# A gated cross-attention and sparse FFN kernel: order of copies, token factors, gates and idle turns

## The chip, the cores and the metric

The kernel runs on one core of one Trainium2 chip. The metric is the device time of one execution in microseconds (us), the median of several runs.

## The reference, cut to what matters

```python
# x, ctx: (32, 128, 512) float32; mask: (32, 128) bool; w_gate, w_up: (512, 2048); w_down: (2048, 512)
def xattn(h, m, mask):
    s = einsum('bsd,bmd->bsm', h, m) / sqrt(512)
    s = where(mask[:, None, :], s, -1e30)
    out = einsum('bsm,bmd->bsd', softmax(s), m)
    return where(any(mask, -1)[:, None, None], out, 0)

def ffn(h):
    g = silu(h @ w_gate) * (h @ w_up)                  # (32, 128, 2048)
    keep, in each group of 4 neighbours, the 2 largest |g|   # 2:4 sparsity
    return g_kept @ w_down

x = x + tanh(g_xattn) * xattn(layernorm(x), ctx, mask)
x = x + tanh(g_ffn)   * ffn(layernorm(x))
```

## The kernel before, in words

Five queues run lists written out by hand, tied by semaphores: SyncE (SP, loads and stores), GpSimd (POOL), ScalarE (ACT), VectorE (DVE) and TensorE (PE). Nothing is planned by a tool; the order in the code is the order on the engine.

**Attention stage.** A loop over 39 slots n; in slot n batch n-1 is turned (four 128x128 transposes of ctx, L1340, four of the normalized x, L1345), batch n-2 gets its scores (L1353, eight passes), batch n-7 is turned for the FFN (L1361), batch n-4 is multiplied with ctx (`av`, L1367) and the probabilities of batch n-3 are turned (`pT`, L1373). ScalarE copies what was turned to SBUF, takes the exponentials and normalizes; VectorE adds the masks, takes maxima and batch statistics and makes `x1`; GpSimd makes powers and reciprocals, and with the time left converts the masks (`CONVERT`), spreads weights (`SPREAD_AT`) and takes differences (`W0_AT`, `X0_AT`). The masks are loaded by broadcast, 128 KB each; so are the two gates, 4 bytes to each of 128 partitions, and ScalarE takes their tanh in slot 3. The identity with which everything is turned is made by GpSimd (L577).

**Products.** The gate and up products are made as a two by two block scheme with seven products instead of eight (`product(u, k, e)`, k = 0 to 6, e = 0, 1), each of six matmuls in two parts: every factor is split in a high part (a rounded copy by ScalarE, `w_high`, `x_high`, `dn_high`, `h_high`) and a low part (what is left, by VectorE or GpSimd, `w_low`, `x_low`, ...). So each factor costs a copy, a subtraction and, for some, a sum (`w_sum`, `x_sum`). The order of the seven token factors is `X_TO`. There are four groups of 1024 tokens (PAIRS = 4), each with four steps s, each step with two units u = 2s and 2s+1; a unit is 14 products, 84 matmuls of about 0.227 us start to start, 19.1 us. From unit 2 on a unit is followed by half of the down product of the step before (`down`, L1399 to L1401, 48 matmuls). A few products of unit 0 stand already in slots 33 to 38 (`EARLY_AT`).

**What hangs on what in a unit.** PE's results lie in PSUM and are collected by ScalarE (`copy_a0`, `copy_a1`, `copy_d0`) and VectorE (`add_c11`, `add_c22`, `add_c12`, `gated0`, `gated1`). PE reuses the banks, so product 2 waits for `copy_a0`, product 4 for `copy_a1`, product 5 for `copy_d0`, product 6 for `add_c22`, and product 0 of the next unit for `gated0`. `x_high_at(s, point)` and `x_low_at(s, point)` put the factors of the next tokens between these. The tokens come from DRAM into `x_blk` (1 MB, L310), `dn_raw` holds raw down weights (L628, issued by GpSimd when the attention stage's stores to `xnT_scratch` have landed, because it takes their place), `w_raw` raw gate and up weights (L288).

Of the kernel before, what the change touches and what calls it, by code (L numbers as in the profile page):

```python
# [5 lines left out]
F32 = mybir.dt.float32  # L6
F32R = mybir.dt.float32r
BF16 = mybir.dt.bfloat16
U8 = mybir.dt.uint8
# [44 lines left out]
CONVERT = {1: 0, 3: 1, 4: 2, 7: 3}  # L54
# [9 lines left out]
PIECE_AT = {6: (0, 2), 7: (0, 3), 11: (1, 0), 12: (1, 1), 28: (1, 2), 29: (1, 3), 36: (2, 0), 37: (2, 1)}  # L64
SPREAD_AT = {5: ((0, 0),), 6: ((0, 1),), 10: ((0, 2),), 11: ((0, 3),), 21: ((1, 0),), 22: ((1, 1),)}
# [66 lines left out]
def flamingo_gated(nc, x, ctx, mask, g_xattn, g_ffn, w_gate, w_up, w_down, out):  # L132
# [9 lines left out]
    with whole:  # L142
# [55 lines left out]
        gates_in = sb("gates_in", [P, 2], F32, 4)  # L198
        ident = sb("ident", [P, P], F32, 4)
        x_blk1 = sb("x_blk1", [P, 4, HALF], F32, 4)  # L200
        mask_in = x1nT[:, 0, 0:2].rearrange("p c n -> p (c n)").bitcast(U8)
# [36 lines left out]
        gates_done = sem("gates_done")  # L238
# [184 lines left out]
        def _(sp):  # L423
# [52 lines left out]
            for b in range(INPUTS):  # L476
# [3 lines left out]
                if b == 4:  # L480
                    for n, g in enumerate((g_xattn, g_ffn)):
                        sp.dma_start(gates_in[:, n:n + 1], g.rearrange("(a n) -> a n", a=1)
                                     .to_broadcast([P, 1])).then_inc(gates_loaded, 16)
# [4 lines left out]
            load_mask(3)  # L488
            for n in range(SLOTS):
# [77 lines left out]
        def _(pool):  # L567
            nc.gpsimd.memset(ident[:], 0.0).then_inc(ident_set, 1)
            nc.gpsimd.memset(stats[:], 1.0).then_inc(stats_set, 1)
            nc.gpsimd.memset(least[:, 0:2], EPS)  # L570
# [88 lines left out]
        def _(act):  # L659
# [9 lines left out]

            for n in range(SLOTS):  # L670
# [21 lines left out]
                if 0 <= b < B:  # L692
# [7 lines left out]
                    else:  # L700
                        if b == 2 * TILES:
                            act.wait_ge(mask_neg_done, B // RING)
# [6 lines left out]
                if 0 <= b < B:  # L709
                    if b == 0:  # L710
                        act.wait_ge(gates_loaded, 32)
                        nc.scalar.activation(xattn_gate[:], gates_in[:, 0:1], ACT.Tanh).then_inc(gates_done, 1)
                        nc.scalar.activation(ffn_gate[:], gates_in[:, 1:2], ACT.Tanh).then_inc(gates_done, 1)
# [721 lines left out]
```

## Time and profile before

| | us |
|---|---|
| median of 3 runs | 1083.94 (1083.72 to 1084.35) |
| the profiled execution's own time | 1086.38 |
| span of its trace, first to last instruction | 1084.6 |
| PE busy | 1070.9 |
| DVE busy | 794.3 |
| ACT busy | 614.3 |
| POOL busy | 226.1 |

PE is TensorE's matmul, PEld its weight load, DVE VectorE, ACT ScalarE, POOL GpSimd, SP SyncE. A row of the timeline gives the start from the span's start, the duration, the engine, the line of the kernel, what is written and read, the count of like instructions in a row, and in brackets how long the engine had been idle and whose work ended that. A matmul's end is modelled, so the distance from one start to the next says more than its duration.

### The profile page before, as it was taken

The numbers are of one execution on the slowest core, as the hardware profiler recorded it, in microseconds if no ns is written. First come the engines' busy times: TensorE is split into PE (matmuls) and PEld (weight loads), VectorE is DVE, ScalarE is ACT, GpSimd is POOL, SyncE is SP. The second block draws the span as 40 slices with busy tenths as digits, with TensorE's granted clock in tenths as the row PEclk, the third lists the DMA queues.
The fourth block names the chain that finished last, engine by engine and source line by source line (L and its number), as shares of the span: only waits on it lengthen the run. The fifth ranks groups of instructions, "written<-read, shape, count | busy, mean of one in ns | idle before, by whom it ended". The sixth has DMA issues, their size and how long they took to land.

```text
span 1084.6 us, 15165 instructions
## 1 busy us (share of the span) xinstructions
PE 1070.9 (99%) x4972; PEld 879.4 (81%) x4972; DVE 794.3 (73%) x1389; ACT 614.3 (57%) x1126; POOL 226.1 (21%) x343
## 2 busy tenths in 40 slices
PE   7999999999999999999999999999999999999998
PEld 6888777888888888878888888878888888888887
DVE  6999879998987676676857576676856464665756
ACT  6999776777755454444544454444544444443452
POOL 7887302222111111100011111110000111111021
PEclk9999999999999999999999999999999999999999
DMA  8999985999989777787899767787798666767727
GB/s 301 323 309 323 350 355 134 329 317 289 289 268 362 174 192 189 175 271 204 241 289 285 185 177 192 180 256 203 237 306 247 153 153 155 192 151 190 199 28 144
DMA packets 89821, 252.65 MB, mean 233 GB/s; under 512 B 9104, under 2 KB 9872, under 8 KB 85648
## 3 DMA queue, kind: packets, MB, share of 16 engines
q1 hardware_dynamic: 68144, 203.45, 53.3%
q0 software_dynamic: 21600, 48.24, 26.1%
q8 instruction: 40, 0.66, 0.3%
q14 instruction: 37, 0.30, 0.1%
HBM read 153.09 MB, written 98.57 MB: 232 GB/s over the span
## 4 chain that ended last, share of the span: by engine, by line
PE 88%; DMA 4%; DVE 3%; ACT 2%; issue 1%; SPq 1%; POOL 0%; DVEq 0%; ACTq 0%; POOLq 0%
PE ps_y L1399 10%; PE ps_y L1401 10%; PE ps_y L1400 10%; PE ps_a L1326 9%; PE ps_a L1330 9%; PE ps_a L1328 9%; PE ps_d L1326 5%; PE ps_d L1330 5%; PE ps_d L1328 5%; PE ps_c L1353 3%; PE ps_y L1367 2%; PE ps_c L1330 2%; PE ps_c L1326 2%; PE ps_c L1328 2%; DMA x_blk<-xnT_scratch 2%; PE ps_a L1345 1%
## 5 line engine op out<-in xcount | busy, mean ns | idle before, releaser
L633 POOL DMA_DIRECT2D out_rows<-y_out x124 | 105.7, 856 | 707.5 <-ACT y_out L785 703.9
L1326 PE MATMUL ps_a<-xm,w_ring 128*128 128x512 f32 x512 | 200.2, 391 | 2.5 <-ACT cp L668 1.5
L1328 PE MATMUL ps_a<-xm,w_ring 128*128 128x512 f32 x512 | 199.6, 390 | 0.0
L1330 PE MATMUL ps_a<-xm,w_ring 128*128 128x512 f32 x512 | 199.5, 390 | 0.0
L785 ACT ACTIVATE y_out<-ps_y,ffn_gate 128x512 f32<-128x512 f32 x124 | 85.1, 688 | 182.7 <-PE ps_y L1401 182.7
L1399 PE MATMUL ps_y<-dn,h_hi 128*128 128x512 f32 x480 | 188.1, 392 | 0.3 <-ACT y_out L785 0.2
L1401 PE MATMUL ps_y<-dn,h_lo 128*128 128x512 f32 x480 | 187.2, 390 | 0.0
L1400 PE MATMUL ps_y<-dn,h_hi 128*128 128x512 f32 x480 | 186.7, 389 | 0.0
L762 ACT ACTIVATE h_hi<-hidden 128x512 fp32r<-128x512 f32 x128 | 73.2, 625 | 82.7 <-DVE hidden L1095 82.6
L1069 DVE TENSOR_TENSOR beats<-h_abs 128x512 bf16<-128x512 f32 x186 | 117.7, 684 | 1.3 <-ACT h_abs L755 1.3
L1326 PEld LDWEIGHTS ps_a<-xm,w_ring 128*128 128x128 f32 x512 | 96.1, 188 | 24.8 <-issue 3.0
L1330 PEld LDWEIGHTS ps_a<-xm,w_ring 128*128 128x128 f32 x512 | 96.1, 188 | 20.3
L1328 PEld LDWEIGHTS ps_a<-xm,w_ring 128*128 128x128 f32 x512 | 96.1, 188 | 20.0
L1037 DVE TENSOR_TENSOR cp<-ps_c,cp 128x512 f32<-128x512 f32 x64 | 43.7, 690 | 90.6 <-PE ps_c L1330 90.6
L1399 PEld LDWEIGHTS ps_y<-dn,h_hi 128*128 128x128 f32 x480 | 90.1, 188 | 21.3 <-ACT y_out L785 2.8
L1401 PEld LDWEIGHTS ps_y<-dn,h_lo 128*128 128x128 f32 x480 | 90.1, 188 | 19.3
L1400 PEld LDWEIGHTS ps_y<-dn,h_hi 128*128 128x128 f32 x480 | 90.1, 188 | 18.9
L1326 PE MATMUL ps_d<-xm,w_ring 128*128 128x512 f32 x256 | 100.0, 391 | 1.6 <-ACT hidden L738 1.5
L1330 PE MATMUL ps_d<-xm,w_ring 128*128 128x512 f32 x256 | 99.7, 389 | 0.0
L1328 PE MATMUL ps_d<-xm,w_ring 128*128 128x512 f32 x256 | 99.6, 389 | 0.0
L755 ACT ACTIVATE h_abs<-hidden 128x512 f32<-128x512 f32 x124 | 74.1, 625 | 28.2 <-DVE hidden L1061 28.2
L1043 DVE TENSOR_TENSOR hidden<-ps_a,hidden 128x512 f32<-128x512 f32 x64 | 43.6, 689 | 57.3 <-PE ps_a L1330 56.8
(122 smaller groups left out, 1872.4 us busy)
## 6 DMA issues: line engine op xcount, KB each, us to landing
w_ring<-w_scratch SPq DMA_DIRECT2D x147, 512.0 KB, 4.3
out_rows<-y_out POOLq DMA_DIRECT2D x124, 256.0 KB, 4.2
w_scratch<-w_ring SPq DMA_DIRECT2D x56, 512.0 KB, 5.9
xm_scratch<-x_out SPq DMA_DIRECT2D x40, 512.0 KB, 5.5
xm<-xm_scratch SPq DMA_DIRECT2D x19, 1024.0 KB, 7.4
w_raw<-in_L_ffn_w_down SPq DMA_DIRECT2D x9, 1024.0 KB, 7.8
x_in<-in_x SPq DMA_DIRECT2D x32, 256.0 KB, 5.2
ctx_in<-in_ctx SPq DMA_DIRECT2D x32, 256.0 KB, 5.4
```

What stands on the lines that cost most here:

```text
L633: nc.gpsimd.dma_start(out[RING * (n // (2 * TILES * QS)) + TILES * ORDER[order] + n % TILES], y_out[:, n % 4], accum_op=ALU.add).then_inc( ...
L755: nc.scalar.activation(abs_of(s, order)[:, j], hidden[:, h, j], ACT.Abs).then_inc(abs_done, 1)
L762: nc.scalar.activation(h_hi[:, h, j], hidden[:, h, j], ACT.Copy).then_inc(h_hi_done, 1)
L785: nc.scalar.activation(y_out[:, n % 4], ps_y[n % 2][:], ACT.Identity, scale=ffn_gate[:]).then_inc(y_copied, 1)
L1037: nc.vector.tensor_tensor(cp[:, e, 0], ps_c[e][:], cp[:, e, 0], ALU.add).then_inc(c11_done[e], 1)
L1069: nc.vector.tensor_tensor(beats[:, PAIR[i, j]], abs_of(s, order)[:, i], abs_of(s, order)[:, j], ALU.is_ge).then_inc(beats_done, 1)
L1326: nc.tensor.matmul(to, w_ring[:, k, e, 0, c], xm[:, k, 0, c], start=begins and c == 0, stop=False, skip_group_check=not begins)
L1328: nc.tensor.matmul(to, w_ring[:, k, e, 0, c], xm[:, k, 1, c], start=False, stop=False, skip_group_check=not begins)
L1330: last = nc.tensor.matmul(to, w_ring[:, k, e, 1, c], xm[:, k, 0, c], start=False, stop=c == 1, skip_group_check=not begins)
L1399: nc.tensor.matmul(to, h_hi[:, h, j, at], right[:, 0, j, columns], start=at_j == 0, stop=False)
L1400: nc.tensor.matmul(to, h_hi[:, h, j, at], right[:, 1, j, columns], start=False, stop=False)
L1401: last = nc.tensor.matmul(to, h_lo[:, h, j, at], right[:, 0, j, columns], start=False, stop=at_j == GROUP - 1)
```

## The change

Seven edits: (1) PE's first three slots are written out in another order, with 12, 10 and 6 transposes of the identity between them, whose result nobody reads; (2) the gates are loaded to one partition by ScalarE's queue and spread by a product with a row of ones; (3) the last eight token factors of the first group are made in slots 30 to 37 instead of 29 to 36, the low halves of the last two on VectorE in unit 0; (4) the four masks lie in the place of `xm`'s last product instead of `x1nT`'s, and the fourth is loaded in slot 14 and converted in slot 21, with spreads and weight pieces moved to make room; (5) the last weight piece and `x_blk` are loaded behind the last `xnT_scratch` store; (6) `copy_a1` and `copy_d0` stand ahead of `dn_high`, spreads and `x_high_at`, and VectorE's `x_low_at(s, 0)` behind `add_c22` in all steps; (7) in unit 0 `gated0` comes ahead of the second `add_c12`.

```diff
-CONVERT = {1: 0, 3: 1, 4: 2, 7: 3}
+CONVERT = {1: 0, 3: 1, 4: 2, 21: 3}
-PIECE_AT = {6: (0, 2), 7: (0, 3), 11: (1, 0), 12: (1, 1), 28: (1, 2), 29: (1, 3), 36: (2, 0), 37: (2, 1)}
-SPREAD_AT = {5: ((0, 0),), 6: ((0, 1),), 10: ((0, 2),), 11: ((0, 3),), 21: ((1, 0),), 22: ((1, 1),)}
+PIECE_AT = {6: (0, 2), 8: (0, 3), 12: (1, 0), 13: (1, 1), 28: (1, 2), 30: (1, 3), 36: (2, 0)}
+SPREAD_AT = {5: ((0, 0),), 7: ((0, 1),), 10: ((0, 2),), 11: ((0, 3),), 22: ((1, 0),), 29: ((1, 1),)}
-         | {29 + 2 * (i - 3) + k: (k, i) for i in range(3, 7) for k in range(2)})
+         | {30 + 2 * (i - 3) + k: (k, i) for i in range(3, 7) for k in range(2)})
+IDLE_TURNS = (12, 10, 6)
...
@@ SP
-                if b == 4:
-                    for n, g in enumerate((g_xattn, g_ffn)):
-                        sp.dma_start(gates_in[:, n:n + 1], g...to_broadcast([P, 1])).then_inc(gates_loaded, 16)
-            load_mask(3)
+                if n == 14:
+                    load_mask(3)
-                if n == SLOTS - 3:
-                    load_x_blk(sp, 1, 0)
+            load_w_piece(sp, nc.sync, 2, 1)
+            load_x_blk(sp, 1, 0)
@@ ACT
+            for n, g in enumerate((g_xattn, g_ffn)):
+                nc.scalar.dma_start(gates_in[:, n:n + 1], g.rearrange("(a n) -> a n", a=1)).then_inc(gates_loaded, 16)
-                        act.wait_ge(gates_loaded, 32)
+                        act.wait_ge(gates_spread, 1)
@@ ACT, step s > 1, first unit
-                        x_high_at(s, 0)
                         copy_d0(u, 0)
                         copy_d0(u, 1)
+                        x_high_at(s, 0)
@@ ACT, unit 1
-                    dn_high(0, 0)
-                    dn_high(0, 1)
                     copy_a1(1, 0)
                     copy_a1(1, 1)
-                    dn_high(0, 2)
-                    dn_high(0, 3)
-                    x_high_at(0, 1)
-                    spread(act, 2, 3)
+                    for j in range(GROUP):
+                        dn_high(0, j)
                     copy_d0(1, 0)
                     copy_d0(1, 1)
+                    spread(act, 2, 3)
+                    x_high_at(0, 1)
@@ ACT, unit 3
+                if s == 1:
+                    copy_d0(u, 0)
+                    copy_d0(u, 1)
                 if building:
                     spread(act, u + 1, 1)
                 x_high_at(s, 2)
-                copy_d0(u, 0)
-                copy_d0(u, 1)
+                if s > 1:
+                    copy_d0(u, 0)
+                    copy_d0(u, 1)
@@ DVE
-                if n == SLOTS - 2:
-                    dve.wait_ge(x_lo_done, 13)
-                    x_low(dve, nc.vector, 0, *X0_AT[n - 1])
-                    if s > QS:
-                        x_low_at(s, 0)
                     add_c22(u, 0)
                     add_c22(u, 1)
                     if s <= QS:
                         dn_low(dve, nc.vector, s - 1)
-                        x_low_at(s, 0)
+                    x_low_at(s, 0)
@@ DVE, unit 0
                     add_c11(0, 1)
+                    dve.wait_ge(x_lo_done, 12)
+                    x_low(dve, nc.vector, 0, 0, 6)
+                    x_low(dve, nc.vector, 0, 1, 6)
                     add_c12(0, 0)
+                    gated0(0, 0)
                     add_c12(0, 1)
+                    gated0(0, 1)
                     w_low(dve, nc.vector, 1, 5)
-                    gated0(0, 0)
-                    gated0(0, 1)
@@ PE (turn_ctx, turn_x and score are the loop's old parts)
+            def idle_turns(count):
+                for i in range(count):
+                    nc.tensor.transpose(ps_av[0][:, 0:P], ident[:], ident[:])
+            idle_turns(IDLE_TURNS[0])
+            turn_ctx(0)
+            idle_turns(IDLE_TURNS[1])
+            turn_x(0)
+            turn_ctx(1)
+            score(0)
+            idle_turns(IDLE_TURNS[2])
+            turn_x(1)
+            turn_ctx(2)
+            score(1)
+            turn_x(2)
+            pe.wait_ge(ones_set, 1)
+            pe.wait_ge(gates_loaded, 32)
+            nc.tensor.matmul(ps_av[1][:, 0:2], ones[:], gates_in[:], start=True, stop=True).then_inc(gates_spread, 1)
+            for n in range(3, SLOTS):
```

## Rows read from the trace of the kernel before

**Rows 1.** The page, busy us (share of the span) and instructions.

```profile
PE 1070.9 (99%) x4972; PEld 879.4 (81%) x4972; DVE 794.3 (73%) x1389; ACT 614.3 (57%) x1126; POOL 226.1 (21%) x343
```

**Rows 2.** Chain of waits at the start: start us, us, what.

```profile
10.61 1.71 PE ps_c L1353 x8
...
16.45 0.89 PE ps_c L1353 x8
```

**Rows 3.** Timeline of the start: start, us, engine, line, operation, count, idle before.

```profile
1.25 0.28 POOL L577 TENSOR_SCALAR_AFFINE_SELECT ident<-ident 128x128 f32<-128x128 f32 x1
...
4.22 1.08 PE L1340 MATMUL ps_a<-ident,ctx_in 128*128 128x128 f32 x4 [4.22 <-DMA ctx_in<-in_ctx]
...
6.81 1.11 PE L1345 MATMUL ps_a<-ident,xn 128*128 128x128 f32 x4 [1.51 <-ACT xn L688]
...
12.75 0.29 DVE L1011 TENSOR_REDUCE neg_max<-neg_scores 128x1 f32<-128x129 f32 x1
...
15.09 0.33 PE L1373 MATMUL ps_d<-ident,probs 128*128 128x128 f32 x1
```

**Rows 4.** Busy us of PE, PEld, DVE, ACT, POOL in a stretch; clock, DMA, GB/s.

```profile
40.00:60.00 20.00, 20.00 (x149) 16.83 (x148) 19.55 (x51) 19.46 (x50) 18.02 (x33) 1.00 0.88 308
```

**Rows 5.** Timeline behind the attention stage, and one stretch as in rows 4.

```profile
117.24 1.30 POOL L390 TENSOR_TENSOR xm<-x_blk,xm 128x512 fp32r<-128x512 f32 x1
...
117.62 0.48 PE L1326 MATMUL ps_a<-xm,w_ring 128*128 128x512 f32 x1
...
122.60 0.53 SPq L499 DMA_DIRECT2D xnT_scratch<-x1nT  x1
...
127.23 0.69 DVE L347 TENSOR_TENSOR w_ring<-w_blk,w_ring 128x512 fp32r<-128x512 f32 x1 [1.45 <-ACT w_ring L343]
...
128.00:136.00 8.00, 7.50 (x34) 5.92 (x33) 7.15 (x12) 5.88 (x9) 1.76 (x3) 1.00 1.04 407
```

**Rows 6.** Timeline of PE, unit 1: the matmuls after waits.

```profile
132.93 0.47 PE L1326 MATMUL ps_a<-xm,w_ring 128*128 128x512 f32 x1 [0.49 <-DVE hidden L1055]
...
145.55 0.47 PE L1326 MATMUL ps_a<-xm,w_ring 128*128 128x512 f32 x1 [1.47 <-ACT cp L668]
...
155.08 0.47 PE L1326 MATMUL ps_a<-xm,w_ring 128*128 128x512 f32 x1 [0.25 <-DVE hidden L1055]
```

**Rows 7.** Timeline of ACT, unit 1, and one issue of POOL.

```profile
134.77 0.63 ACT L385 ACTIVATE x_out<-x_blk 128x512 fp32r<-128x512 f32 x1 [1.37 <-DMA xnT_scratch<-x1nT]
...
135.21 0.59 POOL L628 DMA_DIRECT2D dn_raw<-in_L_ffn_w_down  x1 [4.78 <-DMA xnT_scratch<-x1nT]
...
137.50 1.12 ACT L333 ACTIVATE w_blk<-w_raw 128x512 f32<-128x512 f32 x1 [0.60 <-DMA w_raw<-in_L_ffn_w_up]
...
141.14 0.62 ACT L343 ACTIVATE w_ring<-w_blk 128x512 fp32r<-128x512 f32 x1
...
143.77 1.15 ACT L775 ACTIVATE dn<-dn_raw 128x512 fp32r<-128x512 f32 x2 [2.02 <-DMA dn_raw<-in_L_ffn_w_down]
...
146.82 0.63 ACT L385 ACTIVATE x_out<-x_blk 128x512 fp32r<-128x512 f32 x1
```

**Rows 8.** Timeline of DVE, unit 1.

```profile
148.52 0.69 DVE L353 TENSOR_TENSOR w_blk<-w_blk 128x512 f32<-128x512 f32 x1 [0.18 <-ACT w_blk L333]
...
154.25 0.68 DVE L1055 TENSOR_TENSOR hidden<-ps_a,cp 128x512 f32<-128x512 f32 x1
```

**Rows 9.** Timeline of PE and ACT, units 3 and 12.

```profile
200.06 0.47 PE L1326 MATMUL ps_d<-xm,w_ring 128*128 128x512 f32 x1 [0.30 <-ACT hidden L738]
...
469.57 0.64 ACT L385 ACTIVATE x_out<-x_blk 128x512 fp32r<-128x512 f32 x1 [4.14 <-DMA x_blk<-xnT_scratch]
...
470.83 0.47 PE L1326 MATMUL ps_d<-xm,w_ring 128*128 128x512 f32 x1 [0.59 <-ACT hidden L738]
...
482.16 0.50 PE L1399 MATMUL ps_y<-dn,h_hi 128*128 128x512 f32 x1 [0.17 <-ACT y_out L785]
```

**Rows 10.** The tile x_blk, all six loads.

```profile
DMA to landing us min/median/max: 9.0/9.9/10.5
```

More of the change, by code:

```diff
@@ L722, in _ @@
                 if n in X0_AT:
+                    if X0_AT[n] == (0, 6):
+                        act.wait_ge(mask_neg_done, B // RING)
                     x_high(act, 0, *X0_AT[n])
@@ L1332, in product @@
                 last.then_inc(made[k], 1)
-            for n in range(SLOTS):
-                b = n - 1
-                if 0 <= b < B:
-                    pe.wait_ge(ctx_in_loaded[b % INPUTS], 16 * (b // INPUTS + 1))
-                    wait(pe, cT_copied, b)
-                    for c in range(KC):
-                        last = nc.tensor.transpose(ps_cT[:, c], ctx_in[:, b % INPUTS, c * P:(c + 1) * P], ident[:])
-                    last.then_inc(cT_done, 1)
-                    pe.wait_ge(xn_done, b + 1)
-                    wait(pe, xT_copied, b)
-                    for c in range(KC):
-                        last = nc.tensor.transpose(ps_xT[:, c], xn[:, b % 2, c * P:(c + 1) * P], ident[:])
-                    last.then_inc(xT_done, 1)
-                b = n - 2
-                if 0 <= b < B:
-                    pe.wait_ge(xT_copied, b + 1)
-                    pe.wait_ge(cT_copied, b + 1)
-                    wait(pe, neg_scores_done, b - 1)
-                    for c in range(KC):
-                        last = nc.tensor.matmul(ps_sc[b % 2][:, 0:M], xnT[:, b % 2, c], ctxT[:, b % 2, c],
-                                                start=(c == 0), stop=(c == KC - 1))
-                    last.then_inc(scores_done, 1)
@@ new lines, in turn_ctx, with turn_x @@
+            def turn_ctx(b):
+                pe.wait_ge(ctx_in_loaded[b % INPUTS], 16 * (b // INPUTS + 1))
+                wait(pe, cT_copied, b)
+                for c in range(KC):
+                    last = nc.tensor.transpose(ps_cT[:, c], ctx_in[:, b % INPUTS, c * P:(c + 1) * P], ident[:])
+                last.then_inc(cT_done, 1)
+            def turn_x(b):
+                pe.wait_ge(xn_done, b + 1)
+                wait(pe, xT_copied, b)
+                for c in range(KC):
+                    last = nc.tensor.transpose(ps_xT[:, c], xn[:, b % 2, c * P:(c + 1) * P], ident[:])
+                last.then_inc(xT_done, 1)
@@ new lines, in score @@
+            def score(b):
+                pe.wait_ge(xT_copied, b + 1)
+                pe.wait_ge(cT_copied, b + 1)
+                wait(pe, neg_scores_done, b - 1)
+                for c in range(KC):
+                    last = nc.tensor.matmul(ps_sc[b % 2][:, 0:M], xnT[:, b % 2, c], ctxT[:, b % 2, c],
+                                            start=(c == 0), stop=(c == KC - 1))
+                last.then_inc(scores_done, 1)
+            def idle_turns(count):
+                for i in range(count):
+                    nc.tensor.transpose(ps_av[0][:, 0:P], ident[:], ident[:])
@@ L1356, in _ @@
+            for n in range(3, SLOTS):
+                if 3 < n <= B:
+                    turn_ctx(n - 1)
+                    turn_x(n - 1)
+                if 3 < n < B + 2:
+                    score(n - 2)
                 b = n - 7
@@ L1366, in _ @@
                     wait(pe, x1_done, b - 1)
+                    if b == 1:
+                        pe.wait_ge(gates_done, 2)
                     nc.tensor.matmul(ps_av[b % 2][:], probsT[:, b % 2], ctx_in[:, b % INPUTS], start=True,
```

16 lines of the change are left out of this document (7 added, 9 removed).

## The prediction

> **What bounds the kernel now.** I read the page's busy shares first: PE is busy 1070.9 us of a span of 1084.6 [rows 1]. So no edit that shortens work beside TensorE is worth anything by itself, and at most the 13.7 us in which PE stands can be won. The chain of waits and the timeline of the start show where much of it lies: PE does nothing until 4.22, stands again before 6.81, and reaches its first transposed probabilities only at 15.09 [rows 3]. After that it is full: every 20 us stretch of the attention stage has PE busy 20.00, with ScalarE and VectorE near 19.5 [rows 4]. For the rest I looked along PE's timeline for places where two neighbouring matmuls start further apart than the usual 0.23 us. There are nine such waits of 0.3 us or more that the change can touch: four in unit 1 of the gate and up products (three of them in [rows 6], the fourth at 149.11), one at 200.06, and two pairs of the kind of 470.83 and 482.16 [rows 9], the second pair at 711.89 and 723.22. Below, a wait is counted from start to start less 0.23, and 0.08 is added, because the matmul after a restart is that much slower to follow.
>
> **Part 1, the start: idle turns, another order, gates by TensorE.** Before, PE's clock is at its low level here. The granted clock reads 1.00 in the windows view here too, as in [rows 4], but eight matmuls of the scores take 1.71 us at 10.61 and 0.89 us at 16.45 [rows 2]: 1.2 GHz first, 2.4 GHz later, and what preceded the rise was PE's first stretch without a pause. A turn of 128x128 is thus 0.213 us low and 0.11 us high. The identity is ready at 1.53 (1.25 + 0.28) [rows 3]. Twelve idle turns take 2.56 us from some 1.75 on, so they end at 4.3, when the first context's turns were to begin at 4.22: hidden. Ten more follow at 5.15 and end at 7.3 if the clock is still low; x's turns started at 6.81, so they are up to 0.48 late. I take the clock to be up by about 8, since PE then has worked without a pause since 1.75. Then the scores of batch 0 end at 9.45, six idle turns (0.66) at 10.1, x's second turns run 10.1 to 10.55, x's copy and the next xn follow on ScalarE, the scores of batch 1 end at 12.2, and x's third turns at 12.65, about 1.3 earlier than before. Next in line is probs of batch 0: it needs the maximum, which VectorE ends at 13.04 whatever PE does [rows 3], because its own input is held by the loads. So pT starts at about 13.85 instead of 15.09: 1.24 at best. With a rise at 8.6 I get 0.85, with one after 10.6 nothing, and with the rise where it is now a loss of 1.2 (every added turn stands at 0.213 and x's second turns wait for them). Value: 1.1, ends 1.25 and -1.2. The gates' two broadcast loads leave SP's queue and are issued by ScalarE before its first work, in the time in which it waits for the statistics; the tanh reads the same two columns from PSUM. One small matmul for them stands after x's third turns. Cover for both is that wait; without it they would cost under 1 us once, and I take nothing. The fourth mask load goes from the full first queue to slot 14, its conversion (GpSimd, slot 7 to 21) and the spreads that make room keep one such job a slot; PE is full there, so nothing.
>
> The Trainium skill, "TensorE: Matmul & The Clock Gate", section "Part 1: The HAM clock gate", says the moment of the rise is not tied to the kernel's start and differs from run to run. This trace has one execution and cannot show that; by the rule the term of the start would be between -1.2 and 1.25 from run to run, and the median of runs would hide a part of it. It is the first rival below.
>
> **Part 2, the token factors' sums a slot later.** The eight last token factors move from slots 29 to 36 to slots 30 to 37. The early products on PE keep their slots. The product that needs factor 5 (place 2) starts at 117.62 [rows 5]. That factor's low half is now the one that GpSimd makes at 117.24 for 1.30 us, so it is ready at 118.54 where PE would begin at 117.7: PE stands 0.9. Against it, VectorE has one sum of 128x512 fewer (0.6 to 0.7, as in [rows 8]) before slot 32, and it is full there, so GpSimd's job comes up to 0.6 earlier. Ends -0.9 and -0.3 (not below nothing: PE takes products in order, and the factor cannot be earlier than its copy). Value: -0.4. The two last low halves move behind c11 on VectorE, 1.2 us there; VectorE waits 1.45 for ScalarE behind them before 127.23 [rows 5], which hides them.
>
> **Part 3, unit 1.** The four waits are 0.73, 1.71, 0.83 and 0.49 us (the matmuls before them start at 132.05, 143.69, 148.13 and 154.44) [rows 6]. The first is behind gated0, which now comes one addition earlier: gone. The second and third are copies of ScalarE behind dn's high parts, which wait for dn_raw until 143.77 [rows 7], and behind a spread: both gone as such. But what comes late next? VectorE has a fixed list before gated0 of unit 1, on which PE's next unit waits. It is busy without a pause from 148.52 to 154.25 [rows 8], and its list starts when ScalarE is through with dn's parts, a spread and x_high. ScalarE has no pause from 137.50, where a weight load lands, to its last w_high at 141.14, behind which it is free at 141.66 [rows 7]. From there the new order is two copies (0.95), four dn parts (0.53 each, 2.1), two copies (0.95), the spread (1.04): x_high at 146.70 instead of 146.82 [rows 7], but with all else done. VectorE then has its x_low at 147.37 and its list at 147.97 instead of 148.52. So PE's four waits of 3.76 become one of about 3.2 before unit 2, and the gain is only 0.55. This needs dn_raw by 142.6. It lands at 143.77 now, 8.5 after 135.21, because GpSimd issues it when the last xnT store, issued at 122.60, has landed [rows 5, 7]; that store will have 1.5 MB (x_blk and a weight piece) behind it instead of in front, 3.9 us at 407 GB/s [rows 5], so dn_raw comes by about 140. If it does not, the term is -0.5; if the 0.60 wait at 137.50 [rows 7] goes too, 1.15.
>
> What is moved back pays. x_blk was issued at about 120.5 and is now behind the store, and behind the low half of factor 6, at about 124.6. The loads of x_blk land 9.0 to 10.5 us after issue [rows 10], so at 134.1 to 135.6. ScalarE's x_high waits for it; it ran at 134.77 [rows 7], and 0.60 of slack follows, so up to 135.4 costs nothing. I take nothing; the end is -0.2.
>
> **Part 4, the later units.** At 200.06 copy_d0 now precedes a spread and x_high: the wait of 0.54 goes, but VectorE's x_low, which stands before its c22, comes 0.95 later and c22 is just in time. Value 0.4, ends 0.1 and 0.54. At 470.83 copy_d0 stood behind an x_high that waited 4.14 us for x_blk [rows 9]; now only x_high waits. VectorE's x_low moves behind c22 for the same reason. The wait of 0.83 goes. The one at 482.16 (0.44) comes from the same delay: ScalarE is about 1 us earlier at dn's parts and VectorE 0.5, so it goes too. The pair at 711.89 and 723.22 is 0.38 and 0.40. Sum 1.27 + 0.78 = 2.05, ends 0.8 (only the direct waits go, partly) and 2.05. In the other steps copy_d0 can wait up to 0.8 for PE before x_high; ScalarE is about half idle there, so nothing.
>
> **Sum.** 1.1 - 0.4 + 0.55 + 0.4 + 2.05 = 3.7 us. The profiled execution took 1086.38 (span 1084.6) and would take 1082.7; the three runs have the median 1083.94, so 1080.2.
>
> **Rivals.** (a) The clock rises as late as now. For it: the rise is an observation of one execution; against it: PE is without a pause much earlier. Term 1 is then -1.2: 1082.5. (b) The waits of ScalarE and VectorE only change place: units 1 and later give nothing, because each engine's list stays as long. For it: exactly this happens to most of part 3; against: at 470 ScalarE stood 4.14 us for a load, with nothing else late [rows 9]. Gain 0.7: 1083.2. (c) Unit 1's waits all go, if VectorE's list starts earlier than ScalarE's order allows by my count: 3.2 more, 1077.0. (d) The slower one: x_blk. Both engines' lists in unit 1 hang on ScalarE's x_high at about 134.8. Each us of its landing past 135.4 moves PE by one; from 139.1 the whole gain of 3.7 is lost. A landing at 141.6, 17 us after issue, gives 1086.4. For it: the xnT store before it needed 12 us in this queue (122.60 to about 134.7) [rows 5, 7]; against: all six x_blk loads needed 10.5 or less [rows 10].
>
> **Numbers.** Forecast 0.60, (a) 0.15, (b) 0.12, (c) 0.07, (d) 0.06. The range 1078.9 to 1083.0 holds the forecast with its bounds, (a), and leaves out (b)'s half, (c) and (d). A difference under 0.2% (2.2 us) can't be told from none here. Faster by more needs a time under 1081.8: most of the forecast, (c), a little of (a): 0.66. Within: 0.27. Slower: 0.07.
>
> **What would show it.** Part 1: the first pT before 14.3, scores of batch 0 in 0.9 us. Part 2: PE standing 0.3 to 0.9 before its place 2 product. Part 3: no wait inside unit 1 and one of about 3 us before unit 2. Part 4: no wait at the five later places. Wrong would be: unit 2 starting as late as now after the shift of the start, x_high of ScalarE waiting past 135.4 for x_blk, or new waits above 0.3 us after unit 3.

## The result, and the profile after

The changed kernel takes 1088.48 us (median of 6 runs, 1087.27 to 1089.47) against 1084.58 for the kernel before in the same session: ratio 1.0035, 95% interval 1.0023 to 1.0046. It is slower by 3.9 us; the forecast was 1080.2, faster by 3.7, and the time lies outside its range.

The profiled execution of the changed kernel took 1087.74 (span 1085.9), that of before 1086.38 (span 1084.6). So the two traces differ by 1.3 us where the medians differ by 3.9. A comparison of these two traces alone would mislead; the second profile of before, below, is needed.

**The start.** PE's timeline, columns as in [rows 3]:

```profile
6.86 0.65 PE L1348 MATMUL ps_a<-ident,xn 128*128 128x128 f32 x4
...
8.20 1.16 PE L1356 MATMUL ps_c<-ctxT,xnT 128*128 128x128 f32 x8
9.20 0.82 PE L1363 MATMUL ps_y<-ident 128*128 128x128 f32 x6
...
14.26 0.33 PE L1405 MATMUL ps_d<-ident,probs 128*128 128x128 f32 x1 [1.22 <-ACT probs L685]
```

Scores run at the high level from the first batch on: its eight passes take 1.0 us, from 8.20 to 9.20, where they took 1.71 before [rows 2]. The first pT comes at 14.26 instead of 15.09, and PE stands 1.22 before it. The forecast had 13.85, because it took VectorE's maximum to end at 13.04 as before [rows 3]. It ended at 13.68, behind a load of x that VectorE had at 10.83 (at 10.13 in the trace of before):

```profile
10.83 0.69 DVE L1034 BATCH_NORM_STATS2 bn<-x_in 128x6 f32<-128x512 f32 x1 [2.35 <-DMA x_in<-in_x]
...
13.39 0.29 DVE L1013 TENSOR_REDUCE neg_max<-neg_scores 128x1 f32<-128x129 f32 x1
```

**Place 2 and unit 1.** GpSimd's low half of factor 5, then PE's timeline; these rows answer to [rows 5] and [rows 6]:

```profile
116.41 1.27 POOL L393 TENSOR_TENSOR xm<-x_blk,xm 128x512 fp32r<-128x512 f32 x1
...
117.78 0.47 PE L1329 MATMUL ps_a<-xm,w_ring 128*128 128x512 f32 x1 [0.75 <-issue]
...
150.27 0.47 PE L1329 MATMUL ps_a<-xm,w_ring 128*128 128x512 f32 x1 [1.39 <-DVE hidden L1045]
...
154.67 0.47 PE L1329 MATMUL ps_a<-xm,w_ring 128*128 128x512 f32 x1 [1.42 <-DVE hidden L1057]
```

ScalarE and VectorE in the same stretch; they answer to [rows 7] and [rows 8]:

```profile
142.80 2.19 ACT L778 ACTIVATE dn<-dn_raw 128x512 fp32r<-128x512 f32 x4
144.88 1.07 ACT L741 ACTIVATE hidden<-ps_d 128x512 f32<-128x512 f32 x2
145.84 1.11 ACT L336 ACTIVATE w_blk<-w_raw 128x512 f32<-128x512 f32 x1
146.84 0.64 ACT L388 ACTIVATE x_out<-x_blk 128x512 fp32r<-128x512 f32 x1
```

```profile
147.50 0.69 DVE L393 TENSOR_TENSOR x_out<-x_blk,x_out 128x512 fp32r<-128x512 f32 x1 [1.55 <-ACT x_out L388]
148.11 0.69 DVE L356 TENSOR_TENSOR w_blk<-w_blk 128x512 f32<-128x512 f32 x1
...
149.44 1.28 DVE L1045 TENSOR_TENSOR hidden<-ps_a,hidden 128x512 f32<-128x512 f32 x2
```

The low half is done at 117.68 and PE starts place 2 at 117.78; the row of PE names no releaser for its 0.75. The four waits of unit 1 are gone and two new ones of about 1.6 each (start to start) have come, both for VectorE: one inside the unit, at 150.27, and one before unit 2. ScalarE has dn's parts, copy_d0 and the spread ahead of x_high, which so comes as late as before, at 146.84 (146.82 before). The low half of that factor stands first in VectorE's list, so VectorE waits 1.55 for x_high, and only then does its list go on.

**Step 7.** First VectorE of before, then of after, in the stretch before the second half of down:

```profile
528.82 0.68 DVE L390 TENSOR_TENSOR x_out<-x_blk,x_out 128x512 fp32r<-128x512 f32 x1
529.42 0.69 DVE L403 TENSOR_TENSOR x_blk<-x_blk 128x512 f32<-128x512 f32 x1
530.20 0.69 DVE L1043 TENSOR_TENSOR hidden<-ps_a,hidden 128x512 f32<-128x512 f32 x1
...
539.71 1.28 DVE L1048 TENSOR_TENSOR cp<-ps_d,cp 128x512 f32<-128x512 f32 x2
```

```profile
529.11 0.69 DVE L1045 TENSOR_TENSOR hidden<-ps_a,hidden 128x512 f32<-128x512 f32 x1 [1.30 <-PE ps_a L1333]
...
531.08 0.68 DVE L393 TENSOR_TENSOR x_out<-x_blk,x_out 128x512 fp32r<-128x512 f32 x1
531.68 0.68 DVE L406 TENSOR_TENSOR x_blk<-x_blk 128x512 f32<-128x512 f32 x1
...
539.82 1.28 DVE L1050 TENSOR_TENSOR cp<-ps_d,cp 128x512 f32<-128x512 f32 x2
```

Before, x_low and x_sum (1.2 us together) stood where VectorE waits for PE's product anyway. After, VectorE idles 1.30 there and does them behind c22, in a list without a gap: dn's low parts, the counts, keep, c12. So c12 ends where it did, although PE arrives 1.1 us earlier. PE pays:

```profile
536.03 0.50 PE L1431 MATMUL ps_y<-dn,h_hi 128*128 128x512 f32 x1 [0.15 <-DVE dn L321]
...
542.39 0.50 PE L1431 MATMUL ps_y<-dn,h_hi 128*128 128x512 f32 x1 [0.63 <-ACT y_out L788]
```

The same pair stands at 778.23 and 784.59 (step 11). In steps 6 and 10 the waits ahead of the down product, at 481.04 and 723.24, are 0.60 each. At 470.83, 711.89 and 200.06 PE no longer waits, as forecast for [rows 9].

**The kernel before, profiled again.** A second profile of it has PE at the start, and ScalarE in unit 12, as follows:

```profile
13.84 1.55 PE L1353 MATMUL ps_c<-ctxT,xnT 128*128 128x128 f32 x8
15.22 0.27 PE L1373 MATMUL ps_d<-ident,probs 128*128 128x128 f32 x1
```

```profile
469.00 0.63 ACT L385 ACTIVATE x_out<-x_blk 128x512 fp32r<-128x512 f32 x1 [3.59 <-DMA x_blk<-xnT_scratch]
```

x_blk landed half a microsecond earlier than in [rows 9], and PE's wait at 470 was 0.21 instead of 0.75; the pair at 711.89 and 723.22 was not there. This execution took 1085.18. The waits that part 4 was to remove are thus partly an accident of the first profile: of the experiments below with ScalarE's order of before, e3, e10 and e11 have 0.53 to 0.57 at 470, e12 has 0.35, and e2, e5, e8, e9 and e13 have under 0.2.

Where PE starts some units, in each trace (us):

| kernel | unit 3 | unit 4 | unit 13 | unit 15 | unit 23 | end |
|---|---|---|---|---|---|---|
| before | 185.87 | 216.55 | 487.75 | 547.88 | 788.92 | 1084.56 |
| before, again | 185.79 | 216.50 | 487.21 | 547.34 | 787.70 | 1083.38 |
| after | 185.41 | 215.98 | 486.66 | 548.02 | 790.22 | 1085.87 |
| e1 | 185.32 | 215.88 | 486.62 | 546.97 | 787.92 | 1083.55 |
| e2 | 185.26 | 215.96 | 486.64 | 547.97 | 791.04 | 1086.71 |
| e3 | 186.37 | 217.39 | 488.36 | 548.49 | 789.40 | 1085.06 |
| e6 | 183.72 | 215.86 | 485.94 | 546.29 | 787.06 | 1082.72 |
| e7 | 184.29 | 216.44 | 486.71 | 547.08 | 788.65 | 1084.28 |
| e8 | 183.99 | 214.66 | 484.75 | 544.87 | 785.51 | 1081.18 |
| e10 | 183.54 | 214.22 | 485.25 | 545.38 | 785.97 | 1081.65 |

After and e2 lose 1.2 us between units 13 and 15 against all others, and again before unit 23.

### The profile page after: what moved, and what is told of

Same layout as the page of the kernel before. It is cut to its first block, busy times and chain, and to the rows that moved or that the text cites. A ratio compares the mean times of both kernels' runs of the same rounds, so it can differ in the third digit from the quotient of the medians.

```text
span 1085.9 us, 15227 instructions
## 1 busy us (share of the span) xinstructions
PE 1073.4 (99%) x5002; PEld 881.6 (81%) x5002; DVE 794.7 (73%) x1390; ACT 614.3 (57%) x1126; POOL 225.6 (21%) x343
## 4 chain that ended last, share of the span: by engine, by line
PE 90%; DVE 4%; issue 2%; ACT 2%; DMA 1%; SPq 0%; POOL 0%; DVEq 0%; ACTq 0%; POOLq 0%
PE ps_y L1431 10%; PE ps_a L1329 10%; PE ps_y L1433 10%; PE ps_y L1432 10%; PE ps_a L1331 10%; PE ps_a L1333 10%; PE ps_d L1329 5%; PE ps_d L1331 5%; PE ps_d L1333 5%; PE ps_c L1329 3%; PE ps_c L1333 3%; PE ps_c L1331 3%; PE ps_y L1399 3%; PE ps_c L1356 2%; PE ps_a L1348 1%
```

## The experiments

The ratio is to the kernel before, from runs on the same chip, with its 95% interval. Medians of different sessions differ by some tenths for the same kernel, so I compare ratios; 0.001 is 1.1 us.

| kernel | median | ratio, interval |
|---|---|---|
| after | 1088.48 | 1.0035, 1.0023 to 1.0046 |
| e1 after, x_low back | 1086.81 | 1.0018, 1.0010 to 1.0027 |
| e2 before, x_low behind c22 | 1088.53 | 1.0032, 1.0020 to 1.0044 |
| e3 before, the start alone | 1086.56 | 1.0007, 0.9999 to 1.0016 |
| e4 after, no idle turns | 1089.40 | 1.0043, 1.0027 to 1.0058 |
| e5 e1, part 4 back | 1084.88 | 1.0006, 0.9997 to 1.0015 |
| e6 e1, ScalarE's unit 1 back | 1084.86 | 1.0000, 0.9992 to 1.0009 |
| e7 e1, slots back | 1085.40 | 1.0002, 0.9993 to 1.0010 |
| e8 e1, all three back | 1083.03 | 0.9982, 0.9973 to 0.9991 |
| e9 e8, y first | 1082.58 | 0.9981, 0.9971 to 0.9991 |
| e10 before, loads alone | 1083.28 | 0.9987, 0.9978 to 0.9996 |
| e11 e10, copy_d0 first in step 1 | 1083.34 | 0.9985, 0.9976 to 0.9995 |
| e12 e9, new order in unit 1 | 1083.02 | 0.9978, 0.9969 to 0.9987 |
| e13 e10, with the start | 1083.19 | 0.9984, 0.9975 to 0.9992 |

**e1 and e2: VectorE's x_low.** e1 undoes the edit in the changed kernel, e2 makes it alone in the kernel before:

```diff
-                    if s > QS:
-                        x_low_at(s, 0)
                     add_c22(u, 0)
                     add_c22(u, 1)
                     if s <= QS:
                         dn_low(dve, nc.vector, s - 1)
-                        x_low_at(s, 0)
+                    x_low_at(s, 0)
```

> The changed kernel, with VectorE's x_low and x_sum of the steps after the fourth put back ahead of its two c22 additions. Theory L (the loss is VectorE's: its x_low and x_sum, 1.2 us together, now stand behind c22 and delay keep, silu1 and the copies of y): the waits near 536 and 542 and near 778 and 785 go (2 x 1.1 to 1.3 us), of those at 470 and 711 up to 1.0 comes back, so 1088.5 - 1.5 = 1087.0 (1086.0 to 1087.5), and PE has no wait over 0.3 us near 536 and 542. Rival A (ScalarE's order, copy_d0 ahead of x_high, makes them): both pairs of waits stay and the time stays within 0.5 of 1088.5. Rival S (the loss is at the start, which the traces hide because the profiled execution of before was one of its slow ones): the waits may go, but the time stays over 1087.5.

> The kernel before, with this one part of the change: VectorE's x_low and x_sum behind c22 in the steps after the fourth. Theory L: the waits near 536, 542, 778 and 785 appear and the time is 1084.6 + 2.5 = 1087.1 (1086.0 to 1087.5). Rival A: no such waits, 1084.6 within 0.5. Rival S: 1084.6 within 0.5.

Alone, the edit makes the kernel before slower: ratio 1.0032 (1.0020 to 1.0044), 3.5 us, where theory L had 2.5 and at most 1087.5. Its trace has the waits of the changed kernel at the same places, those ahead of the down product in steps 6 and 10 too (0.60 and 0.76):

```profile
542.37 0.50 PE L1397 MATMUL ps_y<-dn,h_hi 128*128 128x512 f32 x1 [0.63 <-ACT y_out L785]
```

Undone in the changed kernel, the ratio goes from 1.0035 to 1.0018. What PE waits for from 125 to 1050, us in total, times, longest, first after, then e1:

```profile
PE ps_y L1431 <- ACT y_out L788: 2.2, 4, 0.6
PE ps_a L1329 <- DVE hidden L1057: 1.4, 1, 1.4
PE ps_a L1329 <- DVE hidden L1045: 1.4, 1, 1.4
PE ps_y L1431 <- DVE dn L321: 0.3, 2, 0.2
```

```profile
PE ps_a L1331 <- DVE hidden L1045: 1.4, 1, 1.4
PE ps_a L1331 <- DVE hidden L1057: 1.4, 1, 1.4
PE ps_y L1433 <- ACT y_out L788: 0.5, 2, 0.2
```

So theory L holds, rival A (ScalarE's order makes these waits) falls: e1 keeps that order. The cost is 1.8 to 3.5 us by the ratios and 2.3 by the traces of after and e1, of which 0.6 arises in steps 6 and 10 (0.18 and 0.38 in e1 instead of 0.60 each). The profiled execution of e1, 1085.41, is its fastest. Rival S is not excluded for the rest: e1 is still slower than before.

**e3 and e4: the start.** e3 is the kernel before with the idle turns, the order of the first turns and the gates by TensorE; e4 is the changed kernel without the turns.

```diff
# e3, onto the kernel before
-                                     .to_broadcast([P, 1])).then_inc(gates_loaded, 16)
+                nc.scalar.dma_start(gates_in[:, n:n + 1], g.rearrange("(a n) -> a n", a=1)).then_inc(gates_loaded, 16)
+            idle_turns(IDLE_TURNS[0])
...
# e4, onto the changed kernel
-IDLE_TURNS = (12, 10, 6)
+IDLE_TURNS = (0, 0, 0)
```

> The kernel before, with the start of the changed one alone: idle turns, the order of the first turns and scores, and the gates by ScalarE's two loads and a matmul. The mask loads stay where they were. Theory L with the start as the two traces show it: pT of batch 0 comes 0.8 us earlier, 1084.6 - 0.8 = 1083.8. Rival S (the clock of the kernel before rises early in most of its executions, so that the idle turns only stand in the way): 1085.6 to 1087, slower than before.

> The changed kernel with no idle turns, all else as it is. If the turns bring what the two traces show, this is 0.8 us slower than the changed kernel, 1089.3. Rival S: 1.0 to 2.5 us faster than it, 1086.0 to 1087.5, with the first pT earlier than 14.26.

e3 brings its first pT to 13.85, 1.2 earlier than before, and is not faster: 1.0007; its median lies where rival S had it, its pT does not. Its trace shows the loss in unit 1: the wait for dn_raw is longer and TensorE's clock falls behind it. PE's timeline, and then PE's granted clock (the figure 0.75) in a stretch, columns as in [rows 4]:

```profile
145.88 0.67 PE L1327 MATMUL ps_a<-xm,w_ring 128*128 128x512 f32 x1 [2.62 <-ACT cp L667]
146.34 0.63 PE L1329 MATMUL ps_a<-xm,w_ring 128*128 128x512 f32 x1
146.77 0.63 PE L1331 MATMUL ps_a<-xm,w_ring 128*128 128x512 f32 x1
```

```profile
140.00:144.00 4.00, 3.26 (x15) 2.37 (x13) 1.28 (x2) 0.83 (x2) 0.00 (x0) 1.00 1.01 410
144.00:148.00 4.00, 2.12 (x5) 1.72 (x6) 2.52 (x5) 3.90 (x8) 0.00 (x0) 0.75 1.03 417
148.00:152.00 4.00, 4.00 (x16) 3.20 (x15) 3.76 (x7) 1.82 (x3) 0.72 (x1) 0.83 0.94 351
```

After a wait of 2.62 us eight matmuls follow each other at 0.43 us, the low level, instead of 0.23: 1.6 us on top of the wait. Not all of it is lost, since the two waits of before that follow, 0.75 and 0.41, are gone: 0.4 to 0.5 is left. The mean granted clock of a run shows such an execution as 0.998 or 0.997: 7 of the 11 runs of e3, and 9 of the 104 runs of before that stand beside the experiments; those nine took 1085.4 to 1088.2. The four runs of e3 without it took 1085.6 to 1086.7 and are not faster than before either. The wait itself takes most of the gain: dn_raw is issued at 134.30, 0.9 earlier than before, but lands at 144.08, 0.3 later. So an earlier start made a wait for an unmoved load longer, and in most runs the clock added to it. e4 says little about the idle turns: its two slowest runs (1092.7) have the low clock too, and its interval overlaps that of after. In its trace the clock rises at 10.6 without them and pT comes at 14.53 (after: 14.26); it loses 2.0 at a wait near 212, on which more below. Its expectation (1089.3) was met in the number, for other reasons.

**e5, e6, e7: one part undone each, from e1.** e5 puts ScalarE's x_high ahead of copy_d0 again in all later steps; e6 undoes ScalarE's order of unit 1,

```diff
-                    copy_a1(1, 0)
-                    copy_a1(1, 1)
-                    for j in range(GROUP):
-                        dn_high(0, j)
-                    copy_d0(1, 0)
-                    copy_d0(1, 1)
-                    spread(act, 2, 3)
-                    x_high_at(0, 1)
+                    dn_high(0, 0)
+                    dn_high(0, 1)
+                    copy_a1(1, 0)
+                    copy_a1(1, 1)
+                    dn_high(0, 2)
+                    dn_high(0, 3)
+                    x_high_at(0, 1)
+                    spread(act, 2, 3)
+                    copy_d0(1, 0)
+                    copy_d0(1, 1)
```

and e7 puts the token factors in slots 29 to 36 again, with VectorE's last low half where it was. The diffs of e5 and e7:

```diff
                         copy_a1(u, 1)
+                        x_high_at(s, 0)
                         copy_d0(u, 0)
                         copy_d0(u, 1)
-                        x_high_at(s, 0)
...
                 x_high_at(s, 2)
-                if s > 1:
-                    copy_d0(u, 0)
-                    copy_d0(u, 1)
+                copy_d0(u, 0)
+                copy_d0(u, 1)
```

```diff
-         | {30 + 2 * (i - 3) + k: (k, i) for i in range(3, 7) for k in range(2)})
+         | {29 + 2 * (i - 3) + k: (k, i) for i in range(3, 7) for k in range(2)})
```

Beside them stands b_again, the kernel before, unchanged: the second profile shown above.

> The first experiment's kernel (VectorE's x_low back in front of c22), and ScalarE's x_high again ahead of copy_d0 in all later steps, as before the change. Theory P (part 4 of the forecast holds for ScalarE's order): the waits near 199.5, 470 and 711 come back, 1.0 to 1.4 us in all, 1086.8 + 1.2 = 1088.0. Rival Q (with VectorE's x_low ahead of c22 the order of ScalarE decides nothing, since c22 waits for x_low and that for x_high): 1086.8 within 0.4.

> The first experiment's kernel with ScalarE's order in unit 1 as before the change (dn's parts ahead of and between the copies, x_high ahead of the last spread); VectorE's order and the loads stay. By the traces unit 1 stood 3.4 us before and 3.1 after. Theory V (unit 1 hangs on VectorE's list, which starts at ScalarE's last spread and x_high whatever stands before them): 1086.8 within 0.5, waits of 3.1 to 3.6 in unit 1. Rival W (the order itself was the gain): waits of 4 or more, 1087.8 or more.

> The first experiment's kernel with the token factors again in slots 29 to 36, and VectorE's last low half where it was. The wait of 0.9 at the product of place 2 goes. Theory G (what is won ahead of unit 1 is given back there, since ScalarE's and VectorE's lists of unit 1 start from a weight load that lands at 137.5): the waits of unit 1 grow by what place 2 gained, unit 3 starts where it did (185.3), 1086.8 within 0.4. Rival H (it counts): 1085.9, unit 3 at 184.4.

> The kernel before, unchanged, for a second profile of it. The one at hand was of an execution of 1086.4, the median is 1085.1. Theory N (dn_raw lands earlier in other executions): the first pT again at 15.1, and the wait at 145.5 of 1.6 shorter, 0.3 to 1.0, unit 3 at 184.6 to 185.3. Rival S (TensorE's clock rises earlier in other executions): scores of batch 0 in 0.9 us, first pT before 14.3.

All three came out faster than e1, e6 clear of its interval, where theory P had e5 slower, Q, V and G had e5, e6 and e7 the same within 0.4 or 0.5, and W had e6 slower. Only rival H, for e7, came near (1085.9, unit 3 at 184.4). e5: its trace has the wait at 199.69 back (0.49), as P says, but none at 470 and 711. e6: unit 3 starts at 183.72 instead of 185.32, and unit 1 has waits of 0.35, 0.71 and 0.40 instead of 1.61 and 1.56. With the loads moved, the old order of ScalarE is the better one by 1.6 us: its x_high comes at 144.71 instead of 146.72, because copy_d0 and the spread no longer stand ahead of it. e7: the wait of 0.91 at place 2 is gone and unit 3 starts 1.03 earlier; nothing was given back in unit 1. Both traces lose it again later, at one wait (unit 4 starts at 215.86 in e6 and 216.44 in e7, at 215.88 in e1):

```profile
210.24 0.50 PE L1435 MATMUL ps_y<-dn,h_hi 128*128 128x512 f32 x1 [1.45 <-ACT y_out L788]
```

ScalarE and GpSimd of e6 show why:

```profile
207.46 1.11 ACT L336 ACTIVATE w_blk<-w_raw 128x512 f32<-128x512 f32 x1 [3.27 <-DMA w_raw<-in_L_ffn_w_up]
208.47 1.13 ACT L758 ACTIVATE h_abs<-hidden 128x512 f32<-128x512 f32 x2
209.51 1.25 ACT L788 ACTIVATE y_out<-ps_y,ffn_gate 128x512 f32<-128x512 f32 x2
```

```profile
198.03 0.76 POOL L291 DMA_DIRECT2D w_raw<-in_L_ffn_w_up  x1 [4.28 <-ACT w_blk L336]
```

The copies of y stand behind a spread whose weights land 9.4 us after their issue at 198.03, and this issue waits for an earlier spread. Of b_again, theory N was right on the first pT alone: dn_raw landed at 143.70, the wait at 145.5 was 1.56, not shorter, and unit 3 started at 185.79. What was smaller were the waits at 470 and 711, of which N said nothing. Rival S finds nothing in this profile.

**e8, e9, e10.** e8 undoes all three parts together from e1. e9 adds ScalarE's first copy of y ahead of the two absolute values:

```diff
                     spread(act, u + 1, 3)
+                    copy_y(s - 1, 1, 0)
                 for j in second:
                     absolute(s, 0, j)
```

e10 is the kernel before with three lines of part 3:

```diff
-... 36: (2, 0), 37: (2, 1)}
+... 36: (2, 0)}
-                if n == SLOTS - 3:
-                    load_x_blk(sp, 1, 0)
+            load_w_piece(sp, nc.sync, 2, 1)
+            load_x_blk(sp, 1, 0)
...
                     add_c12(0, 0)
+                    gated0(0, 0)
                     add_c12(0, 1)
+                    gated0(0, 1)
                     w_low(dve, nc.vector, 1, 5)
-                    gated0(0, 0)
-                    gated0(0, 1)
```

> All of ScalarE's orders in units 1 and later and the token factors' slots as before the change, with VectorE's x_low back too; what stays of the change are the start, the places of the weight pieces, masks and x_blk, and gated0 one addition earlier. If each undone part counts by itself: unit 3 starts at 182.8, the time is 0.9990 of before, 1083.9. Theory G2 (a gain ahead of unit 3 is given back near 210, where the copies of y stand behind a spread of ScalarE whose weights land at 207 to 208 whatever came before): a wait of 1.5 to 2.4 near 210, 1084.6, as in the kernel with unit 1 alone undone.

> The kernel with three parts undone, and ScalarE's first copy of y ahead of the two absolute values (1.04 us) in the second halves of the first steps. Theory G2: the wait near 210 is 1.0 shorter than in the kernel with three parts undone and the time 1.0 less, 1083.6 or less. Rival (PE waits there for VectorE or for the weights themselves): the wait and the time are the same within 0.3.

> The kernel before, with three lines of part 3 alone: x_blk and the weight piece behind the last xnT store, and gated0 one addition earlier. Theory D (unit 1 of before waits for dn_raw, whose issue waits for that store): dn_raw is issued at 131 instead of 135, the waits of unit 1 are 1.5 instead of 3.4, unit 3 starts at 184.0. The time is then 1.6 less than before, 1083.4, or, by theory G2, 0.3 to 0.6 less with a wait near 211. Rival: dn_raw lands as late as before (the engines that move data are full) and nothing changes.

All three beat the kernel before. e10, by 1.4 us (0.9987, 0.9978 to 0.9996), bears theory D out. It moves two loads and also `gated0`, so the 1.4 is for the three together: the wait of 0.65 at 132.93, which hung on `gated0`, is gone too. Its issue of dn_raw:

```profile
130.13 0.59 POOL L628 DMA_DIRECT2D dn_raw<-in_L_ffn_w_down  x1
```

against 135.21 before [rows 7], and PE's waits from 125 on, which are no longer for dn_raw's chain (`cp L668`, 1.5 before, 0.2 now):

```profile
PE ps_d L1326 <- ACT hidden L738: 1.3, 3, 0.6
PE ps_a L1326 <- DVE hidden L1055: 0.3, 1, 0.3
PE ps_a L1326 <- DVE w_ring L347: 0.2, 1, 0.2
PE ps_a L1326 <- ACT cp L668: 0.2, 1, 0.2
```

dn_raw was issued 5.1 earlier and landed 2.8 earlier, at 140.99. e8 is faster than its expectation by the ratio, though its unit 3 starts at 183.99 and not 182.8: there dn_raw landed 12.4 us after its issue, and PE waited 1.44 for a copy behind it at 143.68. It had no wait near 210, so theory G2 falls as I put it: the landing is not at a fixed time. With the spread ahead of copy_d0 the piece is issued at 197.36, 13.37 behind the start of unit 3 (e6: 14.31), and ScalarE has it at 205.33. e9 could not show a gain where the wait was already gone; its ratio is that of e8.

**e11, e12, e13.** e11 is e10 with copy_d0 ahead of the spread and x_high in step 1; e12 is e9 with spread, copy_d0, x_high in unit 1 in this order and VectorE's x_low behind c22 there; e13 is e10 with the start of e3.

```diff
# e11
+                if s == 1:
+                    copy_d0(u, 0)
+                    copy_d0(u, 1)
                 if building:
                     spread(act, u + 1, 1)
...
# e12, ScalarE
-                    x_high_at(0, 1)
                     spread(act, 2, 3)
                     copy_d0(1, 0)
                     copy_d0(1, 1)
+                    x_high_at(0, 1)
# e12, VectorE
-                    x_low_at(0, 1)
                     w_sum(dve, 2, 0)
                     w_sum(dve, 2, 1)
                     add_c22(1, 0)
                     add_c22(1, 1)
+                    x_low_at(0, 1)
```

> The kernel with the loads of part 3 alone, and one more edit: in the second half of step 1 ScalarE's copy_d0 ahead of the spread and x_high, as the change has it. Theory R (that order takes the wait of 0.5 at 197.8 and gives more back: the spread, and with it the issue of the weight piece that ScalarE needs before the copies of y, comes 0.95 later): the issue is 14.3 behind the start of unit 3 instead of 13.4, PE waits 0.2 to 1.6 near 210, the time is 0 to 1.2 above the kernel with the loads alone, 1084.0. Rival (part 4 as forecast): the wait at 197.8 goes and nothing comes, 1082.9.

> The kernel with three parts undone and the copy of y first, with one new order in unit 1: ScalarE's last spread and copy_d0 ahead of its x_high, VectorE's x_low behind c22. The wait of 0.7 before the product of place 5 (copy_d0 behind x_high and the spread) should shrink to 0.2 and unit 3 start 0.4 to 0.6 earlier, at 182.8: 1082.1. Rival V (unit 1 hangs on the length of VectorE's list only): the waits change place, unit 3 at 183.3, 1082.6.

> The kernel with the loads of part 3 alone, and the start of the change: idle turns, order, gates by TensorE. On its own the start brought nothing (ratio 1.0007). Theory D2 (its gain was lost in unit 1, which waited for dn_raw; with dn_raw issued early it counts): 0.5 to 1.0 less than the kernel with the loads alone, 1082.5. Rival S (the clock of the kernel with the old start rises by itself at 10 in many executions, pT at 14.0, so that the turns bring nothing): 1083.3 within 0.4.

e11: the issue came 14.3 behind unit 3 as theory R says, the wait at 197.8 was gone, and none came near 210, since the piece was there at 204.60. The time is that of e10 (0.9985 and 0.9987). So the order costs only in executions in which that load is slow. All sixteen traces fit this. With copy_d0 first, the issue is 14.3 behind unit 3: where the piece landed 7.8 to 7.9 after its issue (after, e1, e11) PE did not wait near 210, and where it landed 9.4 to 9.8 after (e4, e6, e7) PE waited 1.6 to 2.0. With the spread first, the issue is 13.4 behind, and no wait there was over 0.22, though the landing took up to 9.3 (e3, and e9 and e12, which also have the copy of y first). That the load was slow in most runs of e1 is argued, not shown. e12: the wait before place 5 fell from 0.72 in e9 to 0.20, and that before unit 2 grew from 0.41 to 1.01. The waits changed place, as rival V says, though unit 3 started later than either text had it, at 184.08; the ratio, 0.9978, is not told apart from 0.9981. Its x_high comes at 146.95, as late as in the changed kernel, yet VectorE's list goes on at 146.13, because x_low stands behind c22 there. e13: the start on top of the loads is worth 0 to 0.3 us (0.9984 against 0.9987), so theory D2 (0.5 to 1.0) falls and rival S holds, and the traces say why. The first pT comes at 13.72 in e13; with the old start it comes at 15.09, 15.22 and 15.19 (before, its repetition, e2), but at 14.01 in e10 and 13.71 in e11. PE's timeline of e10:

```profile
10.03 1.11 PE L1353 MATMUL ps_c<-ctxT,xnT 128*128 128x128 f32 x8
...
14.01 0.33 PE L1373 MATMUL ps_d<-ident,probs 128*128 128x128 f32 x1 [0.83 <-ACT probs L682]
```

The eight scores start 0.94 before the next turns, nearly all at the high level: the clock rose at 10.1, with code that is the same up to here as that of before, where it rose at 14.0. In e10 PE had paused until 9.12, 1.0 before the rise; in before it had worked without a pause for 4.6, which is what the prediction saw ahead of the rise. Hence rival S, which b_again seemed to refute, is true in part. By the rule of the Trainium skill that the prediction weighed ("TensorE: Matmul & The Clock Gate", section "Part 1: The HAM clock gate": the moment of the rise differs from run to run) this is expected, and these traces agree: five profiles of one start gave rises from 10.1 to 14.9. The half microsecond to either side that the page gives for it is too little here.

## Why the prediction was wrong, step by step

- **The step that failed** is in part 4: "VectorE's x_low moves behind c22 for the same reason" and "In the other steps ... nothing". I looked at step 6 alone, where x_high waited 4.14 us for x_blk [rows 9], and costed steps 7 and 11 at nothing from ScalarE's idle share. But the list that moved is VectorE's. In steps 7 and 11 it carries an x_sum besides, and the low parts of dn for the same half, so behind c22 there is no gap, while ahead of c22 there is one of 1.3 us. In steps 6 and 10, where the move was taken for a gain, it costs 0.6. Cost in all: 1.8 us by e1, 3.5 by e2, 2.3 by the traces.
- **A second step failed with it**: ScalarE's new orders and the slots stand in parts 2 to 4, which were put at a gain of 2.6 in all. Undoing the orders and slots gains 3.9 by the ratios (e1 to e8), twice what undoing x_low does from after to e1.
- **Part 4, the gain of 0.4 + 2.05.** Three of the five waits went, at 200.06, 470.83 and 711.89, but of the two profiles of before only the one that I read had 0.5 of the 0.75 at 470.83 and the pair at 711.89. The two ahead of the down product grew, at 481.04 and 723.24 (0.60 each, 0.33 and 0.29 before); by e1 and e2 that is x_low's doing. And e5 puts ScalarE's order at a cost of 1.3 instead: behind copy_d0 the spread, and with it the issue of the next weight piece, comes 0.9 later.
- **Part 3, 0.55.** My count of ScalarE's list was right (x_high at 146.70 forecast, 146.84 measured), and the waits of unit 1 went from 3.44 to 3.13, 0.3 instead of 0.55. One of the two left is inside the unit, where I had none. dn_raw landed at 141.57, 10.9 after its issue, where I had taken 8.5 and "about 140"; it was in time all the same. What I missed is what the same loads give with the old order: 1.6 us more (e6). I compared the new order only with the old order and the late dn_raw. Once dn_raw is there in time, copy_d0 and the spread ahead of x_high hold it back by 2.0, and that costs VectorE 1.55 of idle time.
- **Part 2, -0.4.** The wait was 0.91, the end of my range that I had not taken; e7 puts its price at 1.0 in the trace and 1.7 by the ratio.
- **Part 1, 1.1.** 0.83 in this trace. Over all traces the first pT comes at 13.71 to 15.22 with the old start and at 13.72 to 14.44 with the new one, so the term is -0.7 to 1.5 from one execution to the next. Rival (a) did not happen: the clock rose at 5.8 here, and by 7.8 in every trace with the idle turns. What varies is the start of the kernel before, which I had at a fixed time. Where the start does come earlier and the loads stay, as in e3, the wait for dn_raw takes it.
- **Rivals.** (d) did not happen: x_blk landed 9.3 us after its issue and ScalarE took it without a wait. (b), that the waits of ScalarE and VectorE change place, is what happened to unit 1, but it was put at a gain, where a list that is moved out of a gap is a loss. None of my rivals had the place that decided. The range was narrower than its own terms, too: their worst ends (-1.2, -0.9, -0.5, -0.2, 0.1 and 0.8) add up to a loss of 1.9, 1085.8, and it stopped at 1083.0. The measured 1088.48 lies outside even that.

Undone parts added up: from e1, 1.3 (e5), 2.0 (e6) and 1.7 (e7) by the ratios, 5.0 together, against 3.9 for all three at once (e8), so they overlap. So the changed kernel's loss of 3.8 by the ratio is x_low (1.8) and unit 1's order, the slots and ScalarE's order in later steps (3.9), less what the rest brings (2.0 by e8, of which the two loads and gated0 alone bring 1.4). How much of e5's 1.3 is ScalarE's order elsewhere and how much the wait near 210 in executions without a profile stays open. The new places of the masks were not run alone; e8 has them and e13 does not, and their ratios (0.9982 and 0.9984) are not told apart.

The best kernels run are e12 (1083.02, 0.9978), e9 and e8, which are not told apart from each other, nor from e10, e11 and e13. e8 keeps of the change its loads, its masks, its start and gated0, and leaves ScalarE's and VectorE's orders and the slots as they were; e9 and e12 add their own edits. e12 is 2.4 us faster than before by its ratio.

## What to carry to other kernels

Before an instruction is moved on a full engine, look at both places in every iteration that it touches: the one that it leaves may be a gap in which it cost nothing, and what it now stands in front of is what counts, not how busy another engine is. Where several edits are weighed, cost each against the kernel with the others made: two moved loads and one moved addition were worth 1.4 us by themselves, and the reordering that was to go with them cost more than that. And a wait that ends with a transfer should be read in two executions before it is put in a sum.

## What the runs showed of the hardware

- A single wait of 2.62 us on PE, which had been full before it, was followed by eight matmuls at the low level, 1.2 GHz (mean granted clock 0.75 and 0.83 in two stretches of 4 us), which took 1.6 us more, 0.4 to 0.5 of it lost in the end; waits of 1.45, 1.47 and 1.87 us (e6, before, e4) were followed by none.
- The same load landed 7.8 to 9.8 us after its issue from trace to trace, in a stretch (200 to 210) where the DMA share is 1.02 to 1.04 and 375 to 389 GB/s move: the weight piece of unit 4 (issued 197.36, used at 205.33 in e8; issued 200.18, used at 210.00 in e4).
- dn_raw landed 8.5 us after an issue at 135.21 (before) and 10.9 after one at 130.13 (e10), so an issue 5.1 earlier brought it 2.8 earlier.
- TensorE's clock rose at 10.1 to 14.9 us with the same code, and at 5.0 to 7.8 with the idle turns.
